# A sorted mixture of experts: tiles of four quarters of 32 rows in place of tiles of two halves of 64

## The chip, the cores and the metric

The program runs on one core of one Trainium2 chip. Its time is device time in microseconds (us) from start to end of one execution. Engines are named as in the profile: PE is TensorE (PEld its weight loads), DVE is VectorE, ACT is ScalarE, POOL is GpSimd, SP is SyncE. A "q" behind a name (PEldq, ACTq, DVEq, SPq) marks the engine's instruction queue: register, branch and DMA-issuing instructions, which do not count as busy.

## The reference

Two decoder layers on 4 sequences of 256 tokens of width 256, all in float32. The last step of the second layer is a mixture of experts over the 1024 tokens; it alone is touched by the change.

```
NUM_EXPERTS = 32; TOP_K = 4; MOE_INTER = 96; GROUP = 2
NUM_CHUNK = NUM_EXPERTS // GROUP; CHUNK_INTER = 128; SMALL_SCALE = 0.05
...
def _moe(x2d, Wg, Wu, Wd, cw):
    g = jnp.einsum('th,ehi->eti', x2d, Wg)
    u = jnp.einsum('th,ehi->eti', x2d, Wu)
    a = jax.nn.silu(g) * u * cw.T[:, :, None]
    return jnp.einsum('eti,eih->th', a, Wd)
...
w, sel = _routing(x, gate_w)          # softmax weights and the 4 best of 32 experts of each token
cw_large = jnp.zeros((T, NUM_EXPERTS), x.dtype).at[rows, sel].add(w)
cw_small = jnp.zeros((T, NUM_CHUNK), x.dtype).at[rows, sel // GROUP].add(w)
large = _moe(x, Wg, Wu, Wd, cw_large)
small = _moe(x, cWg, cWu, cWd, cw_small)
return (large + SMALL_SCALE * small).reshape(B, S, H)
```

So each of the 4 x 1024 pairs of a token and one of its experts passes the gate and up weights (256 x 192) and the down weights (96 x 256) of its expert, and those of its chunk (256 x 256 and 128 x 256; two neighbouring experts share a chunk). Then come the weighted sum over the 4 pairs, the residual and a layer norm.

## The kernel before

`decoder` runs the layers one after the other. The mixture is its last part: `token_experts` ends with the logits, `route` sorts the pairs, `experts` computes them.

**Sorting (`route`).** The 4096 pairs are sorted by expert, and each expert's pairs are padded to a multiple of HALF = 64 slots. A tile has 128 slots, so it holds two halves, and each half belongs to one expert. The number of tiles is fixed for the worst case: NTILE = (4096 + 32 x 63) // 128 + 1 = 48. DVE makes the tables `in_tile` (128 x 32 x NTILE) and `in_place`, in four parts; POOL multiplies each part of `in_tile` by the pair numbers (L1706), and PE multiplies the two (L1689), which gives each slot its pair. `owner` and `chunk` (one integer for each half) are the expert and the chunk of each half; they are turned into a row by PE (L1680) and lie in `ti_owner` and `ti_chunk`.

**Computing (`experts`).** A software pipeline over tiles, written out by hand for each engine. In its iteration k:

- POOL gathers the 128 token rows of a tile by an indirect DMA (L1897, into `xg`, four buffers) and scatters the results of the tile six behind (L1904, out of `y`).
- PE turns tile k (L1932, `psX`), computes the hidden layer of tile k-1 (L1945, L1948 with the experts' weights, 192 columns; L1952, L1955 with the chunks', 256 columns; `psG`), turns the activations of tile k-2 (L1964, `psA`) and computes the down product of tile k-3 (L1976, L1979, then L1982, L1985; `psD`). Each product is made of two matmuls of 64 rows of output: the first half of the tile on columns 0 to 63 of the array, the second half on columns 64 to 127.
- ACT copies weights for the second half (L2008, `w_in`), copies `psX` to `xt` (L2012), makes silu of tile k-1 (L2018, `sg`), copies the second half's down weights (L2023, `w_out`) and copies `psD` of tile k-3 to `y` (L2030).
- DVE copies the chunks' weights for the second half (L2055, `c_in`; L2070, `c_out`), makes the products of gate and up (L2061, L2063, `a`) and copies `psA` to `aT` (L2075).
- SP does nothing in the loop. It waits for the scatters, then loads the pairs' results (L1914) and stores the output.

PE can read the first half's weights where they lie (`room`, and `W` for `c_out`), at an address from a register, since all experts' weights are in SBUF. The weights of the second half are first copied to a fixed place, at an address from a register of ACT or DVE. Each engine loads those registers from `ti_owner` or `ti_chunk`, eight integers at a time (L1878, TENSOR_LOAD): one load per table and four tiles. Buffers of weights are double: the copy for tile k waits until tile k-2 has used its buffer (`hidden` for `w_in` and `c_in`, `downed` for `w_out` and `c_out`).

Of the kernel before, what the change touches and what calls it, by code (L numbers as in the profile page):

```python
# [9 lines left out]
ALU = mybir.AluOpType  # L10
ACT = mybir.ActivationFunctionType
# [3 lines left out]
P = 128  # L15
# [9 lines left out]
TOPK = 4  # L25
HALF = P // 2
NTILE = (TOPK * NT * P + NE * (HALF - 1)) // P + 1
NHALF = 2 * NTILE
# [1593 lines left out]
def route(nc, c, tiles):  # L1622
# [5 lines left out]
    with ExitStack() as stack:  # L1628
# [23 lines left out]
        over = st.sb("ro_over", [NHALF, NE])  # L1652
        owner = st.sb("ro_owner", [NHALF, 2])
# [9 lines left out]
        def _(pe):  # L1663
# [15 lines left out]
            for n in range(2):  # L1679
                last = nc.tensor.matmul(psN[0:1, (n + 1) * P:(n + 1) * P + NHALF], owner[:, n:n + 1],  # L1680
                                        c["ident"][0:NHALF, 0:NHALF], start=True, stop=True)
# [29 lines left out]
        def _(dve):  # L1711
# [22 lines left out]
            link(nc.vector.tensor_scalar(full[:, :], psN[:, 0:NE], 1.0 / HALF, (HALF - 1) / (2.0 * HALF), ALU.mult,  # L1734
# [11 lines left out]
            link(nc.vector.tensor_scalar(first[:, :], first[:, :], float(HALF), None, ALU.mult))  # L1746
# [6 lines left out]

            link(nc.vector.tensor_scalar(over[:, :], end[0:NHALF, :], c["pairs"][0:NHALF, 0:1], None, ALU.is_lt))
            nc.vector.tensor_reduce(owner[:, 1:2], over.rearrange("p (c g) -> p c g", g=2)[:, :, 1], AX.X, ALU.add)
            nc.vector.tensor_reduce(owner[:, 0:1], over[:, :], AX.X, ALU.add).then_inc(s["owned"], 1)
# [14 lines left out]
            nc.vector.tensor_scalar(tiles.owner[:, :], psN[0:1, P:P + NHALF], NE - 1.0, None, ALU.min)  # L1771
            nc.vector.tensor_scalar(tiles.chunk[:, :], psN[0:1, 2 * P:2 * P + NHALF], NC - 1.0, None,
                                    ALU.min)
# [44 lines left out]
class Tiles:  # L1818


    def __init__(self, st):
        self.owner = st.sb("ti_owner", [1, NHALF], mybir.dt.int32)
        self.chunk = st.sb("ti_chunk", [1, NHALF], mybir.dt.int32)
# [10 lines left out]
def experts(nc, c, X, tiles, W, rows, in_rows, pairs, out, loads):  # L1834
# [4 lines left out]
    with ExitStack() as stack:  # L1839
# [7 lines left out]
        picked = st.sb("ex_picked", [P, TOPK, NT, NE])  # L1847
        w_in = st.sb("ex_w_in", [P, 2, KD, 2 * INTER])
        c_in = st.sb("ex_c_in", [P, 2, KD, 2 * CINTER])
        w_out = st.sb("ex_w_out", [P, 2, D])  # L1850
        c_out = st.sb("ex_c_out", [P, 2, D])
# [13 lines left out]
            "w_in", "c_in", "w_out", "c_out",  # L1865
            "xturned", "xcopied", "hidden", "gated", "acted", "aturned", "acopied", "downed", "ycopied",
            "weighted", "spread", "scaled", "added", "shifted", "applied")}
        came = [st.sem("co_came%d" % t) for t in range(NT)]
# [5 lines left out]
        def owner_of(owners, engine, table, count, half):  # L1874

            at = half - half % 8
# [4 lines left out]
            return owners[table.name, at][half % 8]  # L1881
# [28 lines left out]
        def _(sp):  # L1910
            for v in range(4):
                sp.wait_ge(scattered[v], 16 * (NTILE // 4))
# [10 lines left out]
        def _(pe):  # L1923
            held, owners = {}, {}
            for k in range(NTILE + 3):
                if k < NTILE:
                    held[k] = (owner_of(owners, mybir.EngineType.PE, tiles.owner, NE, 2 * k),
                               owner_of(owners, mybir.EngineType.PE, tiles.chunk, NC, 2 * k))
# [7 lines left out]
                if j is not None:  # L1936
# [421 lines left out]
```

## Time and profile before

| | us |
|---|---|
| median of 3 runs | 936.94 (933.29 to 937.23) |
| the profiled execution, its own time | 934.89 |
| its span, first to last instruction | 933.1 |
| PE busy in the span | 793.6 (85%) |
| DVE, ACT, POOL busy in the span | 570.0, 451.2, 435.9 |
| `route`, from the logits to the tables | about 704 to 729.6 |
| loop of `experts`, gather of tile 0 to the last copy to `y` | 730.7 to 901.3 |
| last scatter, sums, norm, output | 901.3 to 933.1 |

All of a page's times come from the one profiled execution of 934.89 us. Us positions are counted from the start of its span. The loop of `experts` is the stage to read: it is 170 of the 933 us, and nearly all that the change touches runs in it.

### The profile page before, as it was taken

What the parts mean: (1) busy time and instruction counts of PE and PEld (TensorE: products, weight loads), DVE (VectorE), ACT (ScalarE), POOL (GpSimd) and SP (SyncE); (2) the same over time, 40 slices, a digit from 0 to 9 for tenths busy, and PEclk for the clock granted to TensorE, in tenths of its full rate; (3) what the DMA queues carried; (4) which work ended last, traced back from release to release, by engine and by line L of the source; (5) the groups of instructions that cost most, each with busy time, mean ns of one, the idle gap of its engine ahead of it and who ended that gap; (6) DMA issues with size and microseconds to landing.
All of it is one profiled execution on the core that took longest, in us unless ns stands there. A gap on an engine that the chain in (4) does not pass through costs nothing. (4 is left out here: it accounts for less than half of the span.)

```text
span 933.1 us, 16474 instructions
## 1 busy us (share of the span) xinstructions
PE 793.6 (85%) x5043; PEld 502.3 (54%) x5046; DVE 570.0 (61%) x1975; ACT 451.2 (48%) x1438; POOL 435.9 (47%) x395
## 2 busy tenths in 40 slices
PE   6799999976638998799999998995962799999963
PEld 4576666654524443455555554884751455555533
DVE  3666667874784776698888887332538343334445
ACT  2476667654741000688888886000431255545534
POOL 4355546450633665466666664001611466565630
PEclk9879999997977999899999999998875699999986
DMA  9300000000002766200000000601657122222215
GB/s 329 152 1 2 1 2 1 1 1 1 1 0 56 176 159 163 91 1 1 2 1 1 1 2 1 270 1 63 230 154 202 40 70 72 72 69 69 64 51 181
DMA packets 33254, 64.39 MB, mean 69 GB/s; under 512 B 7104, under 2 KB 21836, under 8 KB 32304
## 3 DMA queue, kind: packets, MB, share of 16 engines
q1 hardware_dynamic: 20960, 41.67, 13.8%
q0 software_dynamic: 5664, 13.00, 4.5%
q10 hardware_dynamic: 6544, 8.67, 3.6%
q8 instruction: 43, 0.70, 0.3%
q14 instruction: 43, 0.35, 0.1%
HBM read 42.32 MB, written 10.89 MB: 57 GB/s over the span
## 5 line engine op out<-in xcount | busy, mean ns | idle before, releaser
L285 POOL TENSOR_TENSOR a_Pr<-a_Pr,a_rd 128x1024 f32<-128x1024 f32 x64 | 121.2, 1893 | 68.0 <-DVE a_rd L226 67.8
L258 ACT ACTIVATE a_Pr<-a_Sm,a_nm 128x257 f32<-128x257 f32 x256 | 127.4, 500 | 34.1 <-DVE a_nm L210 33.3
L210 DVE CUSTOM_DVE_ANT_0 a_Sm<-a_psS,table,NSK 128x256 f32<-128x256 f32 x256 | 107.9, 477 | 1.8 <-PE a_psS L159 1.8
L787 ACT ACTIVATE l_Pr<-l_Sm,l_nm 128x128 f32<-128x128 f32 (+1 forms) x192 | 88.3, 461 | 36.2 <-DVE l_nm L690 22.1
L816 POOL TENSOR_TENSOR l_Pr<-l_Pr,l_rd 128x256 f32<-128x256 f32 (+1 forms) x80 | 81.9, 1041 | 49.7 <-DVE l_rd L704 49.5
L159 PE MATMUL a_psS<-room 64*128 64x256 f32 x512 | 74.2, 410 | 5.7 <-DVE a_nm L210 3.8
L1904 POOL DMA_INDIRECT pairs<-ex_y,ti_index x48 | 49.7, 1035 | 58.1 <-ACT ex_y L2030 54.8
L159 PEld LDWEIGHTS a_psS<-room 64*128 64x128 f32 x512 | 45.4, 190 | 57.8 <-issue 48.6
L2061 DVE TENSOR_TENSOR ex_a<-ex_psG,ex_sg 128x96 f32<-128x96 f32 x48 | 12.4, 258 | 99.9 <-ACT ex_sg L2018 99.9
L1361 PE MATMUL p_ps<-p_XT,W 128*128 128x512 f32 x160 | 72.4, 612 | 0.8 <-ACT p_XT L1374 0.8
L1391 DVE SCALAR_TENSOR_TENSOR p_T<-p_ps,BQK,table 128x512 f32<-128x512 f32 x80 | 56.3, 746 | 26.5 <-PE p_ps L1361 26.5
L172 PE MATMUL a_psT<-table,a_Pr 128*128 128x128 f32 x512 | 70.8, 282 | 1.5 <-ACT a_PT L265 1.5
L172 PEld LDWEIGHTS a_psT<-table,a_Pr 128*128 128x128 f32 x512 | 55.5, 142 | 24.9 <-issue 24.1
L184 PE MATMUL a_psO<-a_PT,room 128*64 128x512 f32 x256 | 68.7, 617 | 0.0
L1897 POOL DMA_INDIRECT ex_xg<-rows,ti_index x48 | 49.8, 1038 | 16.3 <-issue 14.5
L914 PE MATMUL o_ps<-W,room 128*128 128x256 f32 x256 | 56.0, 380 | 1.0 <-PEq L114 1.0
L231 DVE COPY a_PT<-a_psT 128x512 f32<-128x512 f32 x64 | 44.3, 692 | 18.5 <-PE a_psT L172 14.8
L712 DVE COPY l_PT<-l_psT 128x384 f32<-128x384 f32 (+1 forms) x48 | 28.7, 598 | 41.9 <-PE l_psT L628 41.7
L914 PEld LDWEIGHTS o_ps<-W,room 128*128 128x128 f32 x256 | 48.5, 190 | 8.2 <-issue 1.9
L1361 PEld LDWEIGHTS p_ps<-p_XT,W 128*128 128x128 f32 x160 | 31.3, 197 | 39.6 <-issue 39.6
L1955 PE MATMUL ex_psG<-ex_c_in,ex_xt 128*64 128x256 f32 x192 | 50.2, 385 | 0.0
L1952 PE MATMUL ex_psG<-room,ex_xt 128*64 x192 | 50.1, 384 | 0.0
(307 smaller groups left out, 1848.6 us busy)
## 6 DMA issues: line engine op xcount, KB each, us to landing
room<-p_E SPq DMA_DIRECT2D x96, 64.0 KB, 2.0
room<-p_E ACTq DMA_DIRECT2D x96, 64.0 KB, 2.0
room<-in_w_in SPq DMA_DIRECT2D x1, 6144.0 KB, 17.3
room<-in_c_in SPq DMA_DIRECT2D x1, 4096.0 KB, 14.2
room<-pairs SPq DMA_DIRECT2D x8, 512.0 KB, 9.1
W<-in_w SPq DMA_DIRECT2D x1, 3072.0 KB, 13.1
room<-in_w_out SPq DMA_DIRECT2D x1, 3072.0 KB, 19.6
W<-in_wo SPq DMA_DIRECT2D x1, 2048.0 KB, 8.6
```

The source lines that it names most:

```text
L159: last = nc.tensor.matmul(psS[:, 2 * (t % 2) + u, qt, :], heads.q(g, n, qt), heads.k(g, n), start=True, stop=True, skip_group_check=True)
L172: last = nc.tensor.transpose(psT[:, u, kt, qt * P:(qt + 1) * P], Pr[:, t % 4, 2 * u + qt, kt * P:(kt + 1) * P], c["ident"])
L184: last = nc.tensor.matmul(psO[h * R:(h + 1) * R, g % 2, :], heads.v(g, h, kt), kept[:, h, kt, :], start=(kt == 0), stop=(kt == 1))
L210: nc.vector.tensor_tensor_reduce(out=Sm[:, t % 2, n, 0:S], in0=psS[:, 2 * (t % 2) + n // 2, n % 2, :], in1=mask[:, n % 2, :], scale=-scale ...
L258: nc.scalar.activation(Pr[:, t % 4, n, :], src, ACT.Exp, bias=nm[:, t % 2, n:n + 1], scale=scale if mask is None else -1.0, accum_out=den[ ...
L285: pool.tensor_tensor(p, p, rd[:, t % 2, :].unsqueeze(2).to_broadcast([P, 4, S]), ALU.mult).then_inc(normed, 1)
L787: nc.scalar.activation(Pr[:, t % 4, n, 0:n_keys], Sm[:, t % 2, n, 0:n_keys], ACT.Exp, bias=nm[:, t % 2, n:n + 1], scale=-1.0, accum_out=de ...
L816: last = pool.tensor_tensor(p, p, r.unsqueeze(2).to_broadcast([P, n, n_keys]), ALU.mult)
L914: last = nc.tensor.matmul(ps[:, t % 4, 0:D], QT[:, i // 2, i % 2, t // 2, (t % 2) * P:(t % 2 + 1) * P], WO1[:, i, :], start=(i == 0), stop ...
L1361: last = nc.tensor.matmul(ps[:, i % 3, e, :], W1[:, k, (2 * g + e) * P:(2 * g + e + 1) * P], XT[:, k, n * 512:(n + 1) * 512], start=(k == ...
L1391: last = nc.vector.scalar_tensor_tensor(out=T[:, i % 2, part, :].rearrange("p (b s) -> p b s", b=2), in0=ps[:, i % 3, e, :].rearrange("p ( ...
L1955: last = nc.tensor.matmul(psG[HALF:P, j % 2, 2 * INTER:2 * (INTER + CINTER)], xt[:, j % 2, kk, HALF:P], c_in[:, j % 2, kk, :], start=(kk = ...
```

## The change

A tile now holds four quarters of Q = 32 slots, each of one expert. Experts are padded to multiples of 32, so NTILE = (4096 + 32 x 31) // 128 + 1 = 40. Each product of PE is made of four matmuls of 32 rows of output, one for each group of 32 columns of the array. PE reads the weights of quarter 0 in place. ACT copies `w_in` for quarters 1 to 3, DVE copies `c_in` and `c_out` for quarters 1 to 3. ACT's copy of `w_out` is gone: SP fetches the three down weights from HBM (`in_w_out`) by three DMAs of 96 rows of 1 KB (96 KB) for each tile, into the space of `CT`, double buffered. `ti_owner` and `ti_chunk` have 160 entries in the order quarter, tile, so that a load of eight serves one quarter of eight tiles: PE needs one load per table and eight tiles, ACT, DVE and SP three loads in a row every eighth tile. In `route` the widths of `in_tile` and of what follows shrink from 48 to 40, and the comparison that makes `owner` runs on 80 rows of two quarters. `picked` now lies in the space of `w_in`, so DVE waits for the last hidden layer before its first use.

```
-HALF = P // 2
-NTILE = (TOPK * NT * P + NE * (HALF - 1)) // P + 1
+Q = P // 4
+NTILE = (TOPK * NT * P + NE * (Q - 1)) // P + 1
...
+            for j in range(NTILE):
+                need(sp, s["downed"], j - 1)
+                for q in (1, 2, 3):
+                    e = owner_of(owners, mybir.EngineType.SP, tiles.owner, NE, j, q)
+                    sp.dma_start(w_out[0:INTER, j % 2, q - 1:q, :],
+                                 out_weights[:, bass.ds(e, 1), :]).then_inc(fetched[j % 2], 16)
...
-                    pe.wait_ge(s["w_in"], j + 1)
+                    pe.wait_ge(s["w_in"], 3 * j + 3)
                     for kk in range(KD):
-                        nc.tensor.matmul(psG[0:HALF, j % 2, 0:2 * INTER], xt[:, j % 2, kk, 0:HALF],
-                                         W.w_in[:, bass.ds(e * KD + kk, 1), :].rearrange("p a n -> p (a n)"),
-                                         start=(kk == 0), stop=(kk == KD - 1))
-                        nc.tensor.matmul(psG[HALF:P, j % 2, 0:2 * INTER], xt[:, j % 2, kk, HALF:P],
-                                         w_in[:, j % 2, kk, :], start=(kk == 0), stop=(kk == KD - 1))
...
+                        for q in range(4):
+                            mine = slice(q * Q, (q + 1) * Q)
+                            w = (W.w_in[:, bass.ds(e * KD + kk, 1), :].rearrange("p a n -> p (a n)") if q == 0
+                                 else w_in[:, j % 2, q - 1, kk, :])
+                            nc.tensor.matmul(psG[mine, j % 2, 0:2 * INTER], xt[:, j % 2, kk, mine], w,
+                                             start=(kk == 0), stop=(kk == KD - 1), skip_group_check=True)
...
-                    pe.wait_ge(s["w_out"], j + 1)
...
+                    pe.wait_ge(fetched[j % 2], 48 * (j // 2) + 48)
...
-                    nc.scalar.activation(w_in[:, k % 2],
-                                         W.w_in[:, bass.ds(held[k] * KD, KD), :], ACT.Copy).then_inc(s["w_in"], 1)
+                    for n in range(3):
+                        nc.scalar.activation(w_in[:, k % 2, n], W.w_in[:, bass.ds(held[n] * KD, KD), :],
+                                             ACT.Copy).then_inc(s["w_in"], 1)
...
-                j = lagging(k, 2)
-                if j is not None:
-                    need(act, s["downed"], j - 1)
-                    nc.scalar.activation(w_out[0:INTER, j % 2, :],
-                                         W.w_out[0:INTER, bass.ds(held.pop(j), 1), :].rearrange("p a n -> p (a n)"),
-                                         ACT.Copy).then_inc(s["w_out"], 1)
...
-                    nc.vector.tensor_copy(c_in[:, k % 2],
-                                          W.c_in[:, bass.ds(held[k] * KD, KD), :]).then_inc(s["c_in"], 1)
+                    for n in range(3):
+                        nc.vector.tensor_copy(c_in[:, k % 2, n],
+                                              W.c_in[:, bass.ds(held[k][n] * KD, KD), :]).then_inc(s["c_in"], 1)
```

The order of instructions shows the same at three places. First PE, in the loop of `experts`, before: the turn of one tile and the expert part of the hidden layer (ISA is the register arithmetic for an address in `room`).

```order
L1932 MATMUL ex_psX<-table,ex_xg 128x128 x2
L1945 ISA
L1945 MATMUL ex_psG<-room,ex_xt 64x192
L1948 MATMUL ex_psG<-ex_w_in,ex_xt 64x192
L1945 ISA
L1945 MATMUL ex_psG<-room,ex_xt 64x192
L1948 MATMUL ex_psG<-ex_w_in,ex_xt 64x192
```

The same place of PE in the changed kernel:

```order
L1949 MATMUL ex_psX<-table,ex_xg 128x128 x2
L1966 ISA
L1966 MATMUL ex_psG<-room,ex_xt 32x192
L1966 MATMUL ex_psG<-ex_w_in,ex_xt 32x192 x3
L1966 ISA
L1966 MATMUL ex_psG<-room,ex_xt 32x192
L1966 MATMUL ex_psG<-ex_w_in,ex_xt 32x192 x3
```

Two matmuls of 64 columns have become four of 32, with as many address computations as before.

Second ACT, one round of its loop in which it also loads registers, before:

```order
L1878 TENSOR_LOAD ti_owner
L2008 ISA
L2008 ACTIVATE ex_w_in<-room 128x384
L2012 ACTIVATE ex_xt<-ex_psX 128x256
L2018 ACTIVATE ex_sg<-ex_psG 128x224
L2023 ISA
L2023 ACTIVATE ex_w_out<-room 96x256
L2030 ACTIVATE ex_y<-ex_psD 128x256
```

And in the changed kernel:

```order
L1888 TENSOR_LOAD ti_owner x3
L2031 ISA
L2031 ACTIVATE ex_w_in<-room 128x384
L2031 ISA
L2031 ACTIVATE ex_w_in<-room 128x384
L2031 ISA
L2031 ACTIVATE ex_w_in<-room 128x384
L2035 ACTIVATE ex_xt<-ex_psX 128x256
L2041 ACTIVATE ex_sg<-ex_psG 128x224
L2047 ACTIVATE ex_y<-ex_psD 128x256
```

Three loads and three copies of `w_in` now stand ahead of the copy to `xt`, and the copy of `w_out` is gone.

Third SP, from its jump into `experts`, before:

```order
L1909 UNCONDITIONAL_BRANCH
L1914 DMA room<-pairs 128x4x256 x8
L1918 DMA out<-room 128x2x256 x4
```

And in the changed kernel, the first of the 40 tiles:

```order
L1919 UNCONDITIONAL_BRANCH
L1888 TENSOR_LOAD ti_owner
L1926 ISA
L1926 DMA CT<-in_w_out 96x256
L1888 TENSOR_LOAD ti_owner
L1926 ISA
L1926 DMA CT<-in_w_out 96x256
L1888 TENSOR_LOAD ti_owner
L1926 ISA
L1926 DMA CT<-in_w_out 96x256
```

SP has three fetches for each tile; in every eighth tile each of them stands behind a load of registers.

## Rows read from the trace of the kernel before

**Rows 1.** Page, busy us and instructions of each engine in the span.

```profile
PE 793.6 (85%) x5043; PEld 502.3 (54%) x5046; DVE 570.0 (61%) x1975; ACT 451.2 (48%) x1438; POOL 435.9 (47%) x395
```

**Rows 2.** Stretches: us; busy PE, PEld, DVE, ACT, POOL; clock, DMA share, GB/s.

```profile
780.00:820.00 40.00, 40.00 (x332) 22.96 (x332) 15.54 (x58) 20.73 (x59) 24.03 (x24) 1.00 0.23 73
```

**Rows 3.** Chain that ended last: start, us, engine, output, line.

```profile
748.77 0.37 PE ex_psX L1932 x2
...
892.32 0.37 PE ex_psX L1932 x2
```

**Rows 4.** The same chain inside one tile.

```profile
800.88 0.15 PE ex_psG L1945
...
801.21 0.21 PE ex_psG L1952
```

**Rows 5.** Route, timeline of POOL and DVE; in brackets idle time before and releaser.

```profile
720.41 1.74 POOL L1706 TENSOR_TENSOR ro_in_tile<-ro_in_tile,table 128x384 fp32r<-128x384 f32 x1 [0.49 <-DVE ro_in_tile L1765]
...
719.15 1.18 DVE L1765 TENSOR_TENSOR ro_in_tile<-table,ro_tile 128x384 fp32r<-128x384 f32 x1
```

**Rows 6.** Timeline of PE, cross attention of layer 0: matmuls of 32 columns (128*32).

```profile
173.08 0.64 PE L648 MATMUL l_psO<-l_PT,CT 128*32 128x256 f32 x8
173.65 0.70 PE L613 MATMUL l_psS<-CTX,X 32*128 32x256 f32 x4
```

**Rows 7.** Line L1945 from 799.0 to 799.5: register instructions in PE's queue.

```profile
L1945 PEldq FUSED_REGOPS  x2: 69/69/69, 799.1 to 799.3; - x2
```

**Rows 8.** Timeline of ACT, one tile of the loop.

```profile
800.09 0.38 ACT L2030 ACTIVATE ex_y<-ex_psD 128x256 f32<-128x256 f32 x1 [0.73 <-PE ex_psD L1985]
800.78 0.52 ACT L2008 ACTIVATE ex_w_in<-room 128x384 f32 x1 [0.32 <-issue]
801.21 0.37 ACT L2012 ACTIVATE ex_xt<-ex_psX 128x256 f32<-128x256 f32 x1
802.12 0.36 ACT L2018 ACTIVATE ex_sg<-ex_psG 128x224 f32<-128x224 f32 x1 [0.54 <-PE ex_psG L1955]
802.51 0.42 ACT L2023 ACTIVATE ex_w_out<-room 96x256 f32 x1
```

**Rows 9.** Timeline of DVE, one tile of the loop, and its first two copies.

```profile
802.51 0.26 DVE L2061 TENSOR_TENSOR ex_a<-ex_psG,ex_sg 128x96 f32<-128x96 f32 x1 [1.95 <-ACT ex_sg L2018]
...
802.88 0.28 DVE L2070 COPY ex_c_out<-W 128x256 f32 x1
803.08 0.42 DVE L2075 COPY ex_aT<-ex_psA 128x256 f32<-128x256 f32 x1
803.41 0.45 DVE L2055 COPY ex_c_in<-room 128x512 f32 x1
...
731.23 0.77 DVE L2055 COPY ex_c_in<-room 128x512 f32 x2 [1.65 <-issue]
```

**Rows 10.** Line L1878, loads of registers: ns min/median/max, first and last start.

```profile
L1878 ACTq TENSOR_LOAD <-ti_owner x12: 537/547/745, 729.9 to 882.1; - x12
L1878 PEldq TENSOR_LOAD <-ti_owner x12: 587/590/604, 729.9 to 879.5; - x12
L1878 DVEq TENSOR_LOAD <-ti_chunk x12: 604/788/848, 730.2 to 881.4; - x12
```

**Rows 11.** Line L1322, 64 KB DMAs issued by SP, and their time to landing.

```profile
L1322 SPq DMA_DIRECT2D room<-p_E x96: 507/592/1847, 293.9 to 368.7; - x96
...
DMA to landing us min/median/max: 1.9/2.0/3.9
```

**Rows 12.** Line L1897, POOL's gathers: in the whole loop, and from 730 to 737.

```profile
L1897 POOL DMA_INDIRECT ex_xg<-rows,ti_index x48: 1006/1039/1123, 730.7 to 884.6; - x48
...
L1897 POOL DMA_INDIRECT ex_xg<-rows,ti_index x5: 1007/1012/1123, 730.7 to 736.1; - x5
```

**Rows 13.** Timeline of PE, turn of tile 1, the last wait before the steady loop.

```profile
734.92 0.69 PE L1932 MATMUL ex_psX<-table,ex_xg 128*128 128x128 f32 x2 [0.62 <-DMA ex_xg<-rows,ti_index]
```

More of the change, by code:

```diff
@@ L1679, in _ @@
             for n in range(2):
-                last = nc.tensor.matmul(psN[0:1, (n + 1) * P:(n + 1) * P + NHALF], owner[:, n:n + 1],
-                                        c["ident"][0:NHALF, 0:NHALF], start=True, stop=True)
+                for j in range(2):
+                    at = P + (2 * n + j) * (NQ // 2)
+                    last = nc.tensor.matmul(psN[0:1, at:at + NQ // 2], owner[:, n, j:j + 1],
+                                            c["ident"][0:NQ // 2, 0:NQ // 2], start=True, stop=True)
             last.then_inc(s["rowed"], 1)
@@ L1770, in _ @@
             dve.wait_ge(s["rowed"], 1)
[L1771 to L1773 removed]
+            for n, (table, most) in enumerate(((tiles.owner, NE - 1.0), (tiles.chunk, NC - 1.0))):
+                nc.vector.tensor_scalar(
+                    table.rearrange("p (h j k) -> p h j k", h=2, j=2),
+                    psN[0:1, P + n * NQ:P + (n + 1) * NQ].rearrange("p (j k h) -> p h j k", j=2, h=2),
+                    most, None, ALU.min)
             dve.wait_ge(s["ordered"], 1)
@@ L1831, in take, with experts @@
         self.sel = spare[:, 3 * n:(3 + TOPK) * n].rearrange("p (k t e) -> p k t e", k=TOPK, t=NT)
-def experts(nc, c, X, tiles, W, rows, in_rows, pairs, out, loads):
+def experts(nc, c, X, CT, tiles, W, out_weights, rows, in_rows, pairs, out, loads):
     with ExitStack() as stack:
@@ L1846, in experts @@
         y = st.sb("ex_y", [P, 4, D])
[L1847 to L1851, printed above, removed]
+        w_in = st.sb("ex_w_in", [P, 2, 3, KD, 2 * INTER])
+        c_in = st.sb("ex_c_in", [P, 2, 3, KD, 2 * CINTER])
+        w_out = CT.rearrange("p b k d -> p (b k d)")[:, 0:6 * D].rearrange("p (s n d) -> p s n d", s=2, d=D)
+        c_out = st.sb("ex_c_out", [P, 2, 3, D])
+        picked = w_in.rearrange("p s n k i -> p (s n k i)")[:, 0:TOPK * NT * NE].rearrange(
+            "p (k t e) -> p k t e", k=TOPK, t=NT)
         G, Z = W.sums()
@@ L1864, in experts @@
             "padded",
-            "w_in", "c_in", "w_out", "c_out",
+            "w_in", "c_in", "c_out",
             "xturned", "xcopied", "hidden", "gated", "acted", "aturned", "acopied", "downed", "ycopied",
             "weighted", "spread", "scaled", "added", "shifted", "applied")}
+        fetched = [st.sem("ex_fetched%d" % i) for i in range(2)]
         came = [st.sem("co_came%d" % t) for t in range(NT)]
@@ new lines, in _ @@
+                    pe.wait_ge(s["c_in"], 3 * j + 3)
+                    for kk in range(KD):
+                        for q in range(4):
+                            mine = slice(q * Q, (q + 1) * Q)
+                            w = (W.c_in[:, bass.ds(ch * KD + kk, 1), :].rearrange("p a n -> p (a n)") if q == 0
+                                 else c_in[:, j % 2, q - 1, kk, :])
+                            last = nc.tensor.matmul(psG[mine, j % 2, 2 * INTER:2 * (INTER + CINTER)],
+                                                    xt[:, j % 2, kk, mine], w,
+                                                    start=(kk == 0), stop=(kk == KD - 1), skip_group_check=True)
@@ L2281, in decoder @@
             route(nc, c, tiles)
-            experts(nc, c, X, tiles, W, rows, in_rows, pairs, out, loads)
+            experts(nc, c, X, CT, tiles, W, w_out, rows, in_rows, pairs, out, loads)
         early.close()
```

88 lines of the change are left out of this document (46 added, 42 removed).

## The prediction, made before the changed kernel ran

> **What bounds the kernel now.** I read the page's busy times first: PE works in 85% of the span, no other engine in more than 61% [rows 1]. That is an average over stages, so next comes the stretch of the loop of `experts`: there PE is busy in all of 40.00 us, DVE in 15.54, ACT in 20.73, POOL in 24.03, at a granted clock of 1.00, which is the 2.4 GHz level, and the DMA engines stand at 23% [rows 2]. Then the chain of waits: from 748.77 to 892.32 it returns to the turn of a tile (L1932) 42 times, so a tile costs 143.55 / 42 = 3.418 us, and in between the chain holds nothing but PE [rows 3]. The loop is bound by PE and by nothing else; its 48 tiles take 164.1 us. Inside a tile the chain advances in rounds: 0.16 us for a round of 192 columns and 0.21 us for one of 256 (a round is both halves, side by side) [rows 4]. A float32 product is two such passes, so the hidden layer is 4 rounds of 0.16 and 4 of 0.21, the down product 4 of 0.21; with two turns of 0.37 and a switch of some 0.15 ahead of each product that gives 0.64 + 8 x 0.21 + 0.74 + 0.3 = 3.4 us.
>
> **Fewer tiles.** 40 instead of 48 is a constant of the program. If a tile keeps its 3.418 us, the loop loses 8 x 3.418 = 27.3 us. Everything else asks whether it keeps it. The mark to hold in mind: the gain is gone when a tile takes 164.1 / 40 = 4.10 us.
>
> **Four matmuls where there were two.** Each streams as many columns as before, so a tile costs the same only if four groups of 32 columns run side by side. The trace has that form: in the cross attention of layer 0, four products of 32 columns and 256 streamed elements are 8 instructions at 173.08, and the next work starts at 173.65, 0.57 us later [rows 6]. Two rounds of 0.21 and the switch are 0.57; two by two it would be 4 rounds, 0.99; one by one, 1.8. So they run four abreast, and I take 3.42 us, with 0.05 either way for the staggered starts and the smaller weight loads: 2 us over 40 tiles.
>
> **Can PE's queue feed that?** A tile has 28 matmuls now (332 in 11.7 tiles [rows 2]), as many weight loads, and will have 2 + 32 + 2 + 16 = 52 of each. The queue's pace shows between two register instructions of L1945, of 0.069 us each, which start at 799.1 and 799.3 with four matmuls and four weight loads between them [rows 7]: (0.2 - 0.07) / 8 = 16 ns each, and with the rounding of both starts at most 29. 104 x 16 ns = 1.7 us, six address computations 0.4, and two register loads of 0.59 per eight tiles 0.15 [rows 10]: 2.3 us of 3.42. At 29 ns it is 3.6 us, which would cost 40 x 0.15 = 6 us of the gain.
>
> **ACT.** Three copies of `w_in` for one, none of `w_out`: 0.38 + 3 x 0.52 + 0.37 + 0.36 = 2.67 us per tile [rows 8], and 3 x 0.547 / 8 = 0.21 of register loads [rows 10]; below 3.42. What matters is when `xt` is ready. It stands behind the copies; it ends at 801.58 now and is wanted at the hidden layer of the next step, 800.04 + 3.42 + 0.37 = 803.8, so 2.2 us to spare. Two more copies at a pitch of 0.43 (800.78 to 801.21) take 0.86 of that. The row shown is a step with one register load; in a step with three, two more take 2 x 0.57 = 1.1. That leaves 1.4 us in seven steps of eight and 0.2 in the eighth. Behind `xt` wait silu, then DVE's products and its `aT`, which have a whole step to spare.
>
> **DVE.** Three `c_in` and three `c_out`. Added without overlap: 0.37 (from L2061 to L2070) + 3 x 0.28 + 0.42 + 3 x 0.45 = 2.98, and 3 x 0.788 / 8 = 0.30 of loads, 3.28 us [rows 9, 10]. By pitch it is less: two copies in a row took 0.77, so one costs 0.34, and a `c_out` costs 0.20 up to the next instruction; then 0.37 + 0.60 + 0.33 + 1.02 = 2.3 us. The nearer row is the pair of copies, since that is what will stand there: 2.6 us with the loads, below PE's 3.42 by either count.
>
> **SP's fetches.** The trace has no fetch of 96 KB in the loop. Nearest is a 64 KB DMA issued by SP: 0.59 us in its queue, landed 2.0 us after its issue, 1.9 to 3.9 [rows 11]. The fetch for tile j waits for the down product of j-2 and is wanted by that of j, the last 1.0 us of a step: 2 x 3.42 - 1.0 = 5.8 us. The third DMA is issued 1.2 to 1.4 us on and lands at 3.4, at worst 5.3. In every eighth tile three register loads stand in between (0.55 to 0.79 each [rows 10]): 5.0 to 5.8, against 5.8. Three fetches are 288 KB per tile, 84 GB/s beside 73 [rows 2]; by bytes the DMA share goes from 0.23 to about 0.5.
>
> **Every eighth step**, then, is tight at three places: `xt` with 0.2 us, the fetch with 0 to 0.8, and PE's own two loads of 1.2 us, while each matmul that waits in its queue now stands for less time. I take 0.4 us for each of the four such steps behind the first, 1.5 us in all (0 to 5).
>
> **Start of the loop.** Tile 1's turn waited 0.62 us for its gather [rows 13]; six fetches (576 KB) now start beside the first gathers. +0.3 us (0 to 2). The first copies of ACT and DVE are hidden by the same wait.
>
> **Route.** POOL's four multiplications of 1.74 us alternate with DVE's `in_tile`, which takes 1.18 us beside POOL for 384 elements [rows 5]. At 320 columns POOL takes 1.45. Each of the four steps loses 0.29; DVE's part may shrink a little, the wider comparison for `owner` and four more small matmuls cost some 0.1. -1.2 us (-0.3 to -1.6). The rest of the kernel, the sums and the norm behind the loop, stays.
>
> **The sum.** -27.3 - 1.2 + 0.3 + 1.5 = -26.7 us. Against the profiled execution that is 934.89 - 26.7 = 908.2; that execution lies 2.05 below the median of 936.94, so against the median it is **910**. Its own range: 2 us for the tile, 0 to 5 for the eighth steps, 2 for the start, 1 for route, and which of the two I measure against: 904 to 916.
>
> **Rival 1: the fetches come late in every tile.** If a fetch lands L us after its issue, the pair of steps must hold 2T - 1.0 = 1.6 + L. At L = 3.9, the worst row, T = 3.25, still hidden; at L = 5, T = 3.8 and the loop takes 152 us: 922. For it: rows of 1 KB, 32 KB apart, beside gathers and scatters. Against it: POOL's gathers also fetch 128 KB by 1 KB rows, and PE waited for none after tile 1 (the chain holds none). 8%. PE's queue at its slow bound gives much the same, 916 to 920: 4%.
>
> **Rival 2, the other side: POOL is shut out by DVE's copies.** DVE will copy for 3 x 0.45 + 3 x 0.28 = 2.19 us per tile from SBUF to SBUF, three times as much as now. POOL works 24.03 / 40 x 3.418 = 2.05 us per tile [rows 2]. If it stood still during each copy, a tile would take at least 2.05 + 2.19 = 4.24 us, the loop 169.6: with route and the start 942. It decides from 4.10 us, so if POOL is stopped in more than 2.05 of these 2.19 us. Against it: a gather took 1.012 us (median) while DVE was nearly idle, and 1.039 in the whole loop with DVE copying for 0.73 us per tile [rows 12]; that is 0.03, not a copy's 0.45. 5%.
>
> The Trainium skill has this as a rule (SBUF — State Buffer, section "Who interferes with whom"): a DVE copy in a two-port mode holds a port pair that it shares with GpSimd for the whole instruction, and GpSimd, which needs it to write the descriptors of its DMAs, is fully blocked. By that rule the loop ends as in rival 2. The rows do not bear it out at today's amount of copying.
>
> **Rival 3: four quarters do not run abreast here.** The row is a burst of 8 instructions; the loop asks for 32 in a row with weight loads between. Two by two, the 12 rounds of a tile (0.64 + 1.68 = 2.3 us) double: T = 5.7, the loop 229 us, 1001. Against it is that the row ran at the full rate in its second pass too. 4%.
>
> That the change does not do what it says is not open: tile count, order and waits are fixed when it is built.
>
> **How the numbers follow.** Forecast 910, 77%. Rival 1 and the slow queue, 916 to 925, 12%. Rival 2, 942, 5%. Rival 3, 1001, 4%. Some wait that I don't see and that eats the whole gain, 2%. The range must leave out no more than 2 in 10: 904 to 922 holds the forecast and most of rival 1. About 0.5%, some 5 us, is what a measurement of this kernel can tell from no change: faster 0.89, same 0.02, slower 0.09.
>
> **What would show it.** In the changed kernel's profile: the turns of a tile in the chain 3.42 us apart, also across steps with register loads (if the eighth are longer, by how much, and whom PE waits for); between them only PE; rounds of four starts, 0.16 and 0.21 us apart; DVE busy near 2.9 us per tile and ACT near 2.7; gathers still near 1.04 us; fetches landed 2 to 3 us after issue; POOL's four multiplications near 1.45 us. I am wrong if PE shows idle time ahead of the down product (fetches), of the hidden layer (`xt`, `w_in`, `c_in`) or of the turn (gathers), or if rounds are longer than now.

## The result, and the profile after

The changed kernel took 911.99 us (median of 4 runs, 910.62 to 913.19), the kernel before 936.72 (4 runs, 933.29 to 937.23): a ratio of 0.974, 95% interval 0.971 to 0.977, 24.7 us less. Forecast were 910 and 904 to 922. When the same kernel ran again beside the experiments, on chip 6, it won only 12 us (e5); that is the second half of this document. The record does not name the chip of this first result. It is called the first chip below; the experiments ran on chips 10 (e1 to e4), 6 (e5 to e8) and 7 (e9 to e12), and whether one of these was the first, at another time, is not known.

The profiled execution took 910.62 us with a span of 908.8, against 934.89 and 933.1. Busy time on the page, to hold against [rows 1], and the stretch that answers to [rows 2], with the same columns:

```profile
PE 768.5 (85%) x5783; PEld 480.9 (53%) x5786; DVE 604.3 (66%) x2095; ACT 456.9 (50%) x1438; POOL 420.9 (46%) x379
```

```profile
780.00:820.00 40.00, 39.27 (x606) 20.30 (x598) 29.63 (x101) 25.55 (x69) 24.71 (x24) 1.00 0.54 166
```

PE still fills the stretch, but for the first time not all of it: 0.7 us are missing. DVE works nearly twice as long as before (29.63 for 15.54), ACT 25.55 for 20.73, and the DMA engines stand at 54% in place of 23%.

The chain of waits through one tile, and at one of the steps with register loads (start, us, what):

```profile
782.22 0.37 PE ex_psX L1949 x2
782.59 0.79 PE ex_psG L1966 x16
783.38 0.86 PE ex_psG L1974 x16
784.24 0.37 PE ex_psA L1983 x2
784.61 0.57 PE ex_psD L1999 x8
785.18 0.43 PE ex_psD L2006 x8
785.62 0.37 PE ex_psX L1949 x2
...
789.01 0.37 issue
789.38 0.41 PE ex_psX L1949 x2
```

From turn to turn it is 785.62 - 782.22 = 3.40 us, with nothing but PE in it. At 789.01 the turn of tile 16 comes 0.37 us late ("issue": PE's queue is still at its two register loads); tiles 8, 24 and 32 show 0.41, 0.35 and 0.50.

The rest of the kernel holds the pieces that the sum did not have right. First the longest waits of PE from 730 to 895 us (what waits and for what; total us, times, longest):

```profile
PE ex_psX L2015 <- DMA room<-pairs: 10.5, 1, 10.5
PE ex_psX L1949 <- DMA ex_xg<-rows,ti_index: 6.1, 2, 5.1
PE ex_psD L1999 <- DMA CT<-in_w_out: 2.1, 2, 1.6
PE ex_psX L1949 <- issue: 1.6, 4, 0.5
```

The third row is new: twice PE waits for fetched down weights, 0.5 us at tile 32 and 1.6 at the last tile. The chain there goes back to SP, whose queue works through three register loads at tile 32 and starts late at the last (why, stands below under "The last tile"):

```profile
853.95 0.56 SPq L1888
854.68 2.77 DMA CT<-in_w_out
857.70 0.64 PE ex_psD L1999 x8
...
876.42 1.95 DMA CT<-in_w_out
878.61 0.64 PE ex_psD L1999 x8
...
884.12 5.89 DMA room<-pairs
```

The last row is the load of the pairs' results behind the loop; it took 7.67 us before. And the lines of the steps that the sum priced (ns min/median/max; for the route, start and us):

```profile
L1926 SPq DMA_DIRECT2D CT<-in_w_out x120: 317/317/1174, 732.7 to 876.4; - x120
L1907 POOL DMA_INDIRECT ex_xg<-rows,ti_index x40: 1007/1039/1179, 732.5 to 861.3; - x40
722.78 1.64 POOL L1708 TENSOR_TENSOR ro_in_tile<-ro_in_tile,table 128x320 fp32r<-128x320 f32 x1 [0.43 <-DVE ro_in_tile L1770]
721.69 1.01 DVE L1770 TENSOR_TENSOR ro_in_tile<-table,ro_tile 128x320 fp32r<-128x320 f32 x1
```

POOL's gathers did not grow by one nanosecond in the median (1039, as in [rows 12]) although DVE now copies three times as much. They do meet: all 34 gathers behind 742 us run beside a copy of `c_in` or `c_out`, for 0.84 us of their 1.04 on average. POOL's scatters have a median of 1026 ns, before 1023.

### The profile page after: what moved, and what is told of

Read it like the earlier page. It is cut to its first block and busy times, and to the rows that moved or that the text cites. A ratio compares the mean times of both kernels' runs of the same rounds, so it can differ in the third digit from the quotient of the medians.

```text
span 908.8 us, 18458 instructions
## 1 busy us (share of the span) xinstructions
PE 768.5 (85%) x5783; PEld 480.9 (53%) x5786; DVE 604.3 (66%) x2095; ACT 456.9 (50%) x1438; POOL 420.9 (46%) x379
## 5 line engine op out<-in xcount | busy, mean ns | idle before, releaser
L2031 ACT ACTIVATE ex_w_in<-room 128x384 f32 x120 | 53.6, 514 | 25.2 <-issue 25.2
L1914 POOL DMA_INDIRECT pairs<-ex_y,ti_index x40 | 42.8, 1071 | 50.6 <-ACT ex_y L2047 46.7
L2073 DVE COPY ex_c_in<-room 128x512 f32 x120 | 45.1, 432 | 7.5 <-issue 7.5
L1907 POOL DMA_INDIRECT ex_xg<-rows,ti_index x40 | 42.2, 1056 | 14.2 <-issue 11.7
L258 ACT ACTIVATION_READ_ACCUMULATOR a_Pr<-a_Sm,a_nm 128x1 f32 x256 | 47.8, 187 | 0.0
```

Source lines behind the costliest of these rows:

```text
L258: nc.scalar.activation(Pr[:, t % 4, n, :], src, ACT.Exp, bias=nm[:, t % 2, n:n + 1], scale=scale if mask is None else -1.0, accum_out=den[ ...
L2031: nc.scalar.activation(w_in[:, k % 2, n], W.w_in[:, bass.ds(held[n] * KD, KD), :], ACT.Copy).then_inc(s["w_in"], 1)
```

## The experiments

They ask three things: is the gain the eight tiles, do the copies and fetches cost anything, and what are the gaps worth that are left. A fourth question came with the first answers. Where turns are counted below, the us from the first to the last turn of a tile are those of the turn's line in the profile. "Before" beside an experiment is the kernel before, run on the same chip.

### e1: 48 tiles again

```diff
-NTILE = (TOPK * NT * P + NE * (Q - 1)) // P + 1
+NTILE = 48
```

> The changed kernel with NTILE fixed at 48 again, everything else of the change kept (quarters of 32 columns, copies for three quarters, fetches by SP); the eight tiles more are empty. Theory A (the gain is the count of tiles times PE's time per tile): eight tiles at the 3.39 us seen in the changed kernel and one more step with register loads at 0.4 us give back 27.6 us: 912.0 + 27.6 = 939.6, 938 to 941, so some 3 us above the kernel before. Theory B (part of the gain comes from elsewhere, route and the sums behind the loop): clearly below 936, down to 930.

Measured: 963.25 us (963.12 to 964.93), ratio to before 1.024 (1.022 to 1.027); before took 940.87 beside it. So the smaller number of tiles is more than the whole gain: without it the change costs 22 us on this chip. But no theory had 963. The turns tell where it went:

```profile
L1949 PE MATMUL ex_psX<-table,ex_xg x96: 272/300/477, 739.5 to 919.5; 128*128 128x128 f32 x96
```

180.0 us for 47 steps, 3.83 each, where the changed kernel had 869.0 - 735.6 = 133.4 us for 39, 3.42 each.

### e2: large down weights copied by ACT

```diff
-                    sp.dma_start(w_out[0:INTER, j % 2, q - 1:q, :], out_weights[:, bass.ds(e, 1), :])...
-                    pe.wait_ge(fetched[j % 2], 48 * (j // 2) + 48)
...
+                    pe.wait_ge(s["w_out"], 3 * j + 3)
...
+                        nc.scalar.activation(w_out[0:INTER, j % 2, n, :], W.w_out[0:INTER, ...], ACT.Copy)...
```

> The changed kernel with SP's fetches undone: ACT copies the large down weights of three quarters from SBUF, as it did for one half. Theory A (each engine's own sum decides; PE stays the bound while it is the largest): ACT then needs 2.67 + 3 x 0.42 = 3.93 us per tile by durations and some 3.4 to 3.6 by pitch, with register loads; the turns of a tile come 3.6 to 4.1 us apart, and the time is 920 to 940 us. Theory B (the fetch only took work off an engine with room to spare): 3.39 us apart, 910 to 913 us.

Measured: 930.61 us (928.09 and 933.14), ratio 0.989 (0.985 to 0.993). ACT was busy 31.48 of 40 us, the DMA share fell to 0.22:

```profile
780.00:820.00 40.00, 39.10 (x543) 19.82 (x537) 24.46 (x91) 31.48 (x94) 20.97 (x21) 1.00 0.22 68
```

PE waits for no down weights in it. The time lies in theory A's 920 to 940 us, but e3 and e4, on the same chip and without ACT's copies, are as slow, so it does not speak for A. Fetching costs no more here than copying by ACT, and ACT has room for all six copies; what they would cost on the first chip stays open.

### e3: one more copy by DVE in each tile

```diff
+                    nc.vector.tensor_copy(idle[:, :], W.c_in[:, 0:KD, :].rearrange("p a n -> p (a n)")...
```

> The changed kernel with one more copy of 128x512 float32 from SBUF to SBUF on DVE in each tile, whose result nobody reads. Rival 2 of the prediction (a DVE copy shuts POOL out for its whole length): POOL's DMA instructions grow with the copying, by 0.2 us or more each against the changed kernel's 1.06 and 1.07, and the wait for gathers appears; T rises towards 4. Theory A (copies cost POOL a few hundredths of a us): POOL's instructions stay below 1.12 us, DVE is busy some 3.3 us per tile, PE's turns stay 3.39 us apart, time within 1.5 us of 912.

Measured: 930.45 us (929.71 and 931.20), ratio 0.989 (0.986 to 0.992). DVE was busy 29.07 of 40 us, and the gathers:

```profile
L1908 POOL DMA_INDIRECT ex_xg<-rows,ti_index x40: 1011/1042/2339, 734.8 to 880.1; - x40
```

A median of 1042 ns with four copies of 512 columns per tile beside the three of `c_out`, 1039 with three, 1039 before with one: POOL is not shut out by this copying, in any amount tried. (One gather of 40 took 2.34 us and one scatter 1.88; the scatters' median is 1028.) So rival 2 fails. The time does not fit theory A either, which had 912; e4 and e5 tell why.

### e4: PE's register loads taken apart

```diff
+                    if k % 8 == 2:
+                        load_ahead(owners, mybir.EngineType.PE, tiles.owner, NE, k, 0)
+                    if k % 8 == 6:
+                        load_ahead(owners, mybir.EngineType.PE, tiles.chunk, NC, k, 0)
```

`load_ahead` loads the registers for the eight tiles that follow.

> The changed kernel with PE's two register loads of every eighth step taken apart and ahead: that of the experts in step 2 of 8, that of the chunks in step 6 of 8. The other engines still do their three in a row. Theory A (the 0.35 to 0.50 us by which every eighth turn of a tile is late is PE's own queue: two loads of 0.6 us behind one another while its queue holds less time of work than before): these four gaps vanish, 1.6 us less, 910.4. Theory B (the gap is ACT's: xt behind three loads and three copies): the gaps stay, 912.

Measured: 930.46 us (929.97 to 931.59), ratio 0.989 (0.987 to 0.991), no gap of PE ahead of a turn any more behind the start of the loop, as theory A said, and yet 18 us above the changed kernel's 912. Four different edits, each some 18 us too slow (or 24, with 48 tiles): what they shared was the chip. Before took 940.87 there, only 4 us more than on the first. Held against e4, which has the changed kernel's 40 tiles on the same chip, the 48 tiles of e1 cost 963.25 - 930.46 = 32.8 us, more than the 27.6 expected.

### e5: the changed kernel itself, on another chip

No edit.

> The changed kernel itself, not altered, beside the kernel before on one chip. In the four runs so far (48 tiles, copies by ScalarE, more copies by VectorE, TensorE's loads spread) the mixture's tile took about 3.9 us where the changed kernel's first profile shows 3.39: in each tile the c_in part of the hidden layer lasts 1.2 to 1.5 us in place of 0.86, behind no semaphore. Theory A, it belongs to the chip or to the placement on it, and not to the edits: the unaltered kernel shows it too when it runs on such a chip, 930 us or so against 940 for the kernel before; on another chip it shows 912 and so do its relatives of this call. Theory B, it belongs to any small shift of the program: the unaltered kernel has 912 us and 3.39 us a tile here, whatever the chip, and the altered ones beside it have 3.9.

Measured: 928.22 us (927.54 to 929.07), before 940.12 beside it, ratio 0.988 (0.986 to 0.989). Theory B falls: the unaltered kernel is slow here too, so it is not the edits. That leaves theory A, the chip or the placement on it; which of them, or the time at which it ran, no run tells apart. Turns, and the chain through a disturbed tile:

```profile
L1949 PE MATMUL ex_psX<-table,ex_xg x80: 272/300/476, 739.5 to 885.3; 128*128 128x128 f32 x80
```

```profile
792.41 0.37 PE ex_psX L1949 x2
792.78 0.79 PE ex_psG L1966 x16
793.57 1.49 PE ex_psG L1974 x16
795.06 0.37 PE ex_psA L1983 x2
795.43 0.57 PE ex_psD L1999 x8
796.00 1.65 PE ex_psD L2006 x8
797.65 0.02 issue
797.67 0.38 ACT ex_y L2047
```

145.8 us in place of 133.4: 12.4 of the 17.9 us by which this execution's span (926.7) is longer lie in the loop. The 16 matmuls of the c_in part take 1.49 us where they took 0.86, with no wait between them. The next row but two reads as if the second part of the down product took 1.65 us. On PE it takes 0.43 as ever; the chain has left PE there and stands until 797.65, when PE's signal that `psD` is done reaches ACT, 1.2 us after the product by its rows. ACT begins 0.02 us later.

### e6, e7, e8: the loads apart, a third buffer, and both

e6 is e4 again. e7 gives the fetched weights a third buffer:

```diff
-                need(sp, s["downed"], j - 1)
+                need(sp, s["downed"], j - 2)
...
-                    sp.dma_start(w_out[0:INTER, j % 2, q - 1:q, :], ...).then_inc(fetched[j % 2], 16)
+                    sp.dma_start(w_outs[j % 3][q - 1][0:INTER], ...).then_inc(fetched[j % 3], 16)
```

e8 has that, and ACT, DVE and SP load their registers at steps 2, 4 and 6 of eight for the eight that follow, PE at steps 2 and 6.

> The kernel of e4 once more, word for word, beside the unaltered one. Theory A (the chip): the same tile period as the unaltered kernel of this call, and a time 0 to 1.6 us below it (its edit takes TensorE's two groups of register loads apart, one of them early, which should close the gaps of 0.35 to 0.50 us at tiles 8, 16, 24 and 32). Theory B (the shift of the program): 930 us beside 912.

> A third buffer for the three fetched down weights (two more thirds in the rest of CT, one in the mask's place, which has no reader any more), so that SyncE waits for the down part of tile j-2 in place of j-1 and a fetch starts one tile earlier. By the changed kernel's chain the waits for fetched weights are 0.5 us at tile 32 and 1.6 us at the last tile, 2.1 in all. If they are late because SyncE may not start: 2.0 us below the unaltered kernel, so about 910 where that has 912. Rival: they are late because the transfer itself is slow behind other traffic, or behind SyncE's register loads at every eighth tile: then less than 0.7 us is won.

> The third buffer of e7 and all register loads spread over the eight steps (TensorE, ScalarE, VectorE and SyncE load one group each at steps 2, 4 and 6 for the eight tiles that follow). Expected sum: 1.6 us of gaps at tiles 8, 16, 24 and 32, and 2.1 us of waits for fetched weights: 908.3 us where the unaltered kernel has 912. Rival: the loads cost as much spread as together, since each step has only some 0.1 us to spare on TensorE's sequencer: then only e7's share is won. By theory B on the stall in the c_in part this one is at 925 or more, being another program than the unaltered one.

Measured, beside e5 with 928.22: e6 928.35 (926.27 to 934.38), e7 927.89 (926.25 to 931.22), e8 926.39 (925.60 to 928.04). The longest waits of PE from 730 to 895 in e5, in e7 and in e8, without the shorter ones that the views list behind them:

```profile
PE ex_psX L1949 <- DMA ex_xg<-rows,ti_index: 6.2, 2, 5.5
PE ex_psD L1999 <- DMA CT<-in_w_out: 3.2, 3, 1.4
```

```profile
PE ex_psX L1953 <- DMA ex_xg<-rows,ti_index: 6.3, 2, 5.3
PE ex_psG L1970 <- ACT ex_w_in L2035: 2.5, 2, 1.2
PE ex_psX L1953 <- issue: 1.5, 4, 0.5
```

```profile
PE ex_psX L1965 <- DMA ex_xg<-rows,ti_index: 6.2, 2, 5.4
PE ex_psA L1999 <- issue: 0.8, 2, 0.4
```

Both edits do what they are for: the 3.2 us of waiting for fetches are gone in e7, and in e8 the gaps at the turn are gone too. A third buffer would hide a slow transfer as well as a late start, so e7 alone does not say which it was. The chain of the changed kernel does: its two transfers that PE waited for took 2.77 and 1.95 us, and what came late was their start. The time hardly moved: not at all by e6, 0.3 us by e7, where waits for ACT's `w_in` (2.5 us) stand in place of the fetches, and 1.8 by e8, whose interval (0.985 to 0.988) overlaps that of e5. The expected 2.0 and 3.7 us were worked out where nothing else disturbed the loop. Here other waits take their place. e8 is the fastest of the four, not proven faster, and none of these edits was tried on the first chip.

### e9 to e12: what the lost time goes with

The kernel before, unaltered (e9). The w_in part with one matmul for the whole tile (e10), both parts so (e11; both leave out the weights of quarters 1 to 3), and the w_in part in two halves of 96 columns (e12). The edits of e10 and e12:

```diff
-                        for q in range(4):
-                            nc.tensor.matmul(psG[mine, j % 2, 0:2 * INTER], xt[:, j % 2, kk, mine], w, ...)
+                        w = W.w_in[:, bass.ds(e * KD + kk, 1), :].rearrange("p a n -> p (a n)")
+                        nc.tensor.matmul(psG[:, j % 2, 0:2 * INTER], xt[:, j % 2, kk, :], w, ...)
```

```diff
-                            nc.tensor.matmul(psG[mine, j % 2, 0:2 * INTER], xt[:, j % 2, kk, mine], w, ...)
+                            for part in (slice(0, INTER), slice(INTER, 2 * INTER)):
+                                nc.tensor.matmul(psG[mine, j % 2, part], xt[:, j % 2, kk, mine], w[:, part], ...)
```

> The kernel before, with a profile, on a chip of the experiments. On two chips the changed kernel took 928 to 930 us and before 940 to 941, in place of 912 and 936.7 on the chip of the first result: before lost 4 us there and the changed kernel 16 to 18. In the changed kernel's tiles TensorE stands still for 0.3 to 0.6 us among the 32 plain instructions (16 weight loads, 16 matmuls) of the c_in part, behind no semaphore, and its sequencer reaches the wait behind them up to 1.5 us after the register operation ahead of them, where that never took over 0.15 us on the first chip. Theory T1, TensorE's instructions reach its sequencer too slowly there: before issues 56 of them in a tile of 3.42 us in place of 104, so its tiles show no such stop and keep 3.42 us; what it loses lies elsewhere. Theory T2, the array or its operands are disturbed, whatever the number of instructions: before's tiles are longer too, by 0.3 us or more.

> In the w_in part of the hidden layer one matmul of the whole tile with the first quarter's weights (4 x 128 columns) in place of four abreast (16 x 32 columns): 24 instructions of TensorE fewer in a tile, 80 in place of 104, at the same matrix time of about 0.79 us (the outputs of three quarters are then of the wrong expert). T1 (supply of instructions): on a chip where the unaltered kernel has 3.8 to 3.9 us a tile this one has 3.4 to 3.5, and the time falls by 10 to 15 us. T2: 3.8 to 3.9 us a tile as before. On a chip like the first, both give 3.4 us and 911.

> The same in both parts of the hidden layer: 48 instructions of TensorE fewer in a tile, 56 as in the kernel before (outputs of three quarters of the wrong expert and of the wrong chunk). T1: no stops, 3.39 us a tile, about 912 us whatever the chip. T2: 3.8 to 3.9 us a tile on the slower chips, 926 us or more.

> The w_in part in two halves of 96 columns: 32 instructions of TensorE more in a tile, 136 in place of 104, the same products. T1: if instructions come at the pace that the slower chips show (some 114 with waits and register operations in 3.8 us, 30 per us), a tile takes 146/30 = 4.9 us there, so 40 us more than the unaltered kernel; on a chip like the first it tells how far that one is from the same limit. T2: a tile grows only by what the shorter matmuls cost the array, 0.1 to 0.4 us.

The split of e12 changes what is left in `psG` (its outputs differ from the kernel's, and why was not looked for), so its time stands for the instructions alone. All four ran on chip 7, where before took 940.74 beside them. The mean step counts the short first steps too; steady steps of before take 3.42 us and those of the changed kernel 3.39, on the first chip.

| kernel | median us | matmuls and weight loads per tile | first to last turn, us | mean step, us |
|---|---|---|---|---|
| before, first chip | 936.72 | 56 | 158.8 | 3.38 |
| e9 before | 940.83 | 56 | 161.7 | 3.44 |
| changed, first chip | 911.99 | 104 | 133.4 | 3.42 |
| e5 changed | 928.22 | 104 | 145.8 | 3.74 |
| e11 | 921.93 | 56 | 142.2 | 3.65 |
| e10 | 932.54 | 80 | 146.5 | 3.76 |
| e12 | 938.47 | 136 | 153.4 | 3.93 |

Neither theory stands as it was put. T1 (PE gets its instructions too slowly) wanted 3.4 to 3.5 us per tile in e10, no stops in e11 and 4.9 us in e12, 40 us above the changed kernel. e10 has 3.76 per step with 24 instructions fewer, e11 still has 3.65, though its undisturbed tiles are down to 3.11, and e12 is 0.2 above e5 and not 1.1. T2 (PE's array is disturbed) wanted longer tiles in e9, and there nearly all take 3.42 us. The waits of ACT show what both had missed. What ACT waited for from 760 to 900, in the kernel before on the first chip and in e9 (total us, times, longest):

```profile
ACT ex_sg L2018 <- PE ex_psG L1955: 35.4, 41, 1.1
ACT ex_y L2030 <- PE ex_psD L1985: 29.5, 41, 0.7
```

```profile
ACT ex_y L2030 <- remote: 30.5, 17, 2.4
ACT ex_sg L2018 <- PE ex_psG L1955: 24.6, 15, 2.4
ACT ex_sg L2018 <- remote: 9.5, 4, 2.6
```

"remote" is a wait whose signal is in the trace, but so long after the end of every instruction that could have given it that the profile names none. On the first chip ACT never has one and never stands still for over 1.1 us; in e9 it has 21, about one in every second tile, of 0.9 to 2.6 us. One such tile in the timeline of ACT, first chip and e9:

```profile
820.59 0.38 ACT L2030 ACTIVATE ex_y<-ex_psD 128x256 f32<-128x256 f32 x1 [0.73 <-PE ex_psD L1985]
```

```profile
823.53 0.38 ACT L2030 ACTIVATE ex_y<-ex_psD 128x256 f32<-128x256 f32 x1 [2.37 <-remote]
```

And the last matmuls in e9 of the product that this copy waits for and of the next hidden layer, with the chain at the same place:

```profile
820.71 0.38 PE L1985 MATMUL ex_psD<-ex_c_out,ex_aT 128*64 128x256 f32 x1
822.74 0.38 PE L1955 MATMUL ex_psG<-ex_c_in,ex_xt 128*64 128x256 f32 x1
```

```profile
821.16 2.35 another core or an unknown queue
823.51 0.02 issue
823.53 0.38 ACT ex_y L2030
```

So ACT does not stop by itself. It waits for PE's signal `downed`, which comes at 823.51, and begins 0.02 us later, as it does on the first chip. What is late is the signal: by its rows the product is done at 821.09. In all 21 waits ACT begins 0.02 us behind the signal, and the signal is 1.5 to 2.5 us behind the matmul's end; in the kernel before on the first chip it is 0.02 us behind it in every tile. For `downed` in the changed kernel the delay is 0.04 us in every tile behind 742 us on the first chip, and in e5 1.4 us in the median and up to 2.0. PE's work goes on meanwhile: in e9 its signals `downed`, `xturned`, `hidden` and `aturned` reach the others at 823.51, 823.55, 823.71 and 823.75, though by the rows the matmuls before them end at 821.09, 821.46, 823.12 and 823.49. The 1.7 us of work between the second and the third cannot have been done in 0.16 us, so it is the signals that were held back there, and not the matmuls.

On these chips, then, something on PE's side is late: its signals to ACT and DVE, and now and then its next weight load, by up to 0.5 us in the middle of 32 instructions that wait for nothing (in e5 its sequencer reaches the next wait up to 1.5 us after the register operation ahead of them; on the first chip it took 0.15, once 0.30). The kernel before is a loop in which ACT and DVE have time to spare, and its loop takes 161.7 - 158.8 = 2.9 us longer; the steps show it only where register loads come on top (in the second half of the loop every fourth tile takes 3.81 in place of 3.42). The changed kernel has less room on both engines and pays 12.4 us. That the room is the reason is argued from this table, not shown by an edit. With PE's instructions cut to 56 (e11) the late signals stay. What ACT waited for in e11 from 730 to 895:

```profile
ACT ex_sg L2035 <- remote: 13.8, 6, 3.2
ACT ex_y L2041 <- remote: 11.5, 7, 2.0
```

What holds the signals back stays open. The page's instruction transfers are hardly slower there: the 16 KB ones took 1.08 us on average in the loop of the changed kernel on the first chip and 1.11 in e5, and 1.05 and 1.19 in the kernel before and in e9. The Trainium skill (Runtime: NRT & Kernel Launch, section "Instruction fetch mechanics") says that an engine's sequencer fetches its program in blocks of 16 KiB while it runs, and that this is mostly hidden. No run here ties the late signals to such a block: in e9 they come about every 7 us, these transfers every 12 to 16. Nor is it settled that it is the chip and not what else was set up on it at the time, or the recording of the profile itself: the traces of these chips also lack records of signals (of ACT's `gated`, 8 for 34 tiles in e5 from 742 to 870, 37 for 37 on the first chip).

## Why the prediction was right, point by point

**The whole.** Profiled execution against profiled execution it is -24.3 us, forecast -26.7. The pieces, each from one event in the trace to the next:

| piece | forecast | measured |
|---|---|---|
| all ahead of `route` (code unchanged) | 0 | +2.6 |
| `route`, tile numbers to the first gather | -1.2 | -0.7 |
| first gather to the turn of tile 1 | +0.3 | +0.5 |
| turn of tile 1 to the last copy to `y` | -25.8 | -23.5 |
| behind the loop | 0 | -3.1 |

So the sum came out well in part because two pieces that it did not have nearly cancel: +2.6 in code that was not touched (1.5 to 1.8 of it in the first 43 us, in the loads of the inputs) and -3.1 behind the loop.

**Eight tiles fewer: right.** 8 x 3.418 = 27.3 us; e1 turns the constant back and loses 32.8 us against e4 on the same chip. Eight steps of e4's 147.2 / 39 = 3.77 us are 30.2 of that, and the longer steps of e1 most of the rest.

**The tile keeps its time: right, and a little better.** 3.393 us between undisturbed turns, 0.025 less than 3.418, 1.0 us over 40 tiles. Four quarters run abreast: the 0.57 us of eight instructions that [rows 6] showed stand again in the loop, "0.57 PE ex_psD L1999 x8". Rival 3 is gone.

**PE's queue: right on the first chip.** 104 instructions per tile go through with no gap but in the steps with register loads. e12's 136 take 3.44 us in its one undisturbed steady tile; on the first chip it did not run.

**ACT and DVE: near.** ACT 25.55 / 40 x 3.39 = 2.2 us per tile, forecast 2.67 added without overlap; DVE 29.63 / 40 x 3.39 = 2.5, forecast 2.6 with the loads. The cover held on the first chip. What the forecast did not ask is what it costs when PE's signals come late: `xt` had, by the forecast, 1.4 us to spare in seven steps of eight and 0.2 in the eighth, and the signals of e5 are 1.4 us late in the median and up to 2.0.

**Every eighth step: the right steps, a term too small.** Forecast 0.4 at each of four, 1.5 us; measured 0.41, 0.37, 0.35 and 0.50, 1.6 in all, and it is PE's own two loads in each. The fetch came 0.5 late at tile 32 on top. SP's slack of "0 to 0.8" was about right, its DMA instruction too dear (0.59 taken from [rows 11], 0.317 measured).

**The last tile: not seen.** With no hidden layer left to compute, the last steps are shorter than 3.4 us, so the fetch, which starts when the down product of tile j-2 is done, no longer has its 5.8 us: PE waits 1.6. The step that failed is "wanted by that of j, the last 1.0 us of a step", which holds only in the steady loop. e7 takes these waits away. From the last turn to the last copy to `y` it is 11.2 us where it was 9.1; between the turns the loop lost 25.7 us, as forecast, so nearly all of the 2.3 us by which this piece of the table is off lie in this tail.

**Start of the loop.** Forecast +0.3, measured +0.5: the first gather landed after 3.26 us in place of 2.78, beside six fetches. The clock reached its 2.4 GHz level at 743.5 in place of 740.7, but tile 1's turn came 2.35 us later too, so that cost little: its turn to that of tile 4 took 10.50 us for 10.36.

**Route: half.** POOL's multiplication over 320 columns takes 1.63 us and not 1.45. It shrank by 6% where the columns shrank by 17%; why is open. DVE's part went from 1.18 to 1.01.

**Behind the loop: not priced.** -3.1 us, of which 1.0 is the last scatter that no longer stands behind another, and 1.8 the load of the pairs (5.89 for 7.67).

**Rival 1** (fetches late in every tile) fell on the first chip: 2.1 us in two places. **Rival 2** (POOL shut out by DVE) fell everywhere: gathers of 1039 ns before and after, 1042 in e3. By the rule of the Trainium skill that the prediction weighed (SBUF — State Buffer, "Who interferes with whom"), POOL would have stood still for each copy. No run here agrees with it, at any of the amounts of copying tried, though gathers and copies overlap for 0.84 us on average.

**What the prediction could not see** is that its 3.42 us hold where PE's signals come at once, and that was luck. In e5 on chip 6 the same kernel took 928.22 us, 16 us above the first result and outside the range of 904 to 922, and e4, which differs by two register loads, took 930.46 on chip 10. Nothing in the sum has a term for that.

## What to carry to other kernels

A constant of the program that sets how often a full tile is computed (here padding of 32 in place of 64) is worth its tiles times their steady price, as long as every other engine stays below the bound; and the ends of the loop, where steps are short, need a look of their own for buffers that are timed by a full step. Idle time of engines that are not the bound may still do work: the kernel before, with much of it, lost 4 us where signals came late and the changed kernel 16, so that half of the gain was left; that the one comes from the other is argued, not shown. Run a kernel that uses up that time on more than one chip before you believe the last 2%, and run the unaltered kernel beside every set of edits: e1 to e4 looked like failures of their edits until e5. And ask of a wait whether the engine stood still or its signal came late: a chain that stands for 2.35 us and ends 0.02 us ahead of a copy says that it was the signal.

## What the runs showed of the hardware

- Four float32 matmuls of 32 columns each run abreast in a long loop as they do in a burst: 16 of them, of 256 streamed elements, in 0.86 us.
- With PE's queue full, 104 instructions and six address computations pass in 3.39 us per tile.
- A DMA of 96 rows of 1 KB costs SP 0.317 us in its queue, less than the 0.59 of a 64 KB one in the same kernel.
- DVE's float32 copies in SBUF and POOL's gathers run beside one another: 1039 ns (median) of a gather before and after, with all gathers of the steady loop overlapping copies.
- On chips 10, 6 and 7 signals of PE reached ACT late: `downed` 1.4 us in the median behind the last matmul in e5 and 0.04 on the first chip, at a granted clock of 1.00 in the stretch. ACT began 0.02 us behind the signal in both. PE had stops of up to 0.5 us between two weight loads there, and none on the first chip. The cause is open.
